# Another order of the steps up to the first scores in a cross-attention block

## The reference

```
q, kv = ln(x)*g_q + b_q, ln(ctx)*g_kv + b_kv
qp = q @ Wq.T + bq ; kp = kv @ Wk.T + bk ; vp = kv @ Wv.T + bv
scores = qh @ kh.T / sqrt(32) - spatial_scale[h]*dist(query_xy, token_xy) + spatial_offset[h]
scores = where(mask, scores, -inf)
x = x + softmax(scores) @ vh @ Wo.T + bo
h = ln(x)*g_m + b_m
return x + gelu(h @ W1.T + b1) @ W2.T + b2
```

## Time and profile before

| | us |
|---|---|
| median of 3 runs | 1246.89 (1246.64 to 1247.19) |
| the profiled execution's own time | 1248.32 |
| its span, first to last instruction | 1246.5 |
| TensorE busy | 1205.4 (97%) |
| VectorE busy | 995.8 (80%) |
| ScalarE busy | 855.0 (69%) |
| GpSimd busy | 1000.9 (80%) |
| mean granted TensorE clock | 0.994 |

### The profile page before, as it was taken

How to read it: one execution, slowest core, us unless ns; L and a number is a source line. 1 busy time by engine, 2 the same in 40 slices (tenths; PEclk the granted TensorE clock), 3 DMA queues, 4 the chain that set the end, 5 groups by cost and what they waited for, 6 DMA issues and landing times.

```text
span 1246.5 us, 27428 instructions
## 1 busy us (share of the span) xinstructions
PE 1205.4 (97%) x9258; PEld 782.5 (63%) x9258; DVE 995.8 (80%) x2656; ACT 855.0 (69%) x1918; POOL 1000.9 (80%) x1286
## 2 busy tenths in 40 slices
PE   7887889999999999999999999999999999999998
PEld 2333456666666666666666666666666676666664
DVE  6799998888888989888888987978888887778321
ACT  6877758776767667776767677776767776676331
POOL 5587989989898988979898998989898987768320
PEclk8999999999999999999999999999999999999999
DMA  8599999989899898989899998889999997779543
GB/s 236 156 201 204 246 205 203 203 184 208 198 207 217 180 212 188 212 190 202 195 208 215 179 226 187 198 195 205 201 204 206 195 211 176 167 176 176 145 115 122
DMA packets 469692, 241.67 MB, mean 194 GB/s; under 512 B 385056, under 2 KB 409904, under 8 KB 469552
## 3 DMA queue, kind: packets, MB, share of 16 engines
q1 hardware_dynamic: 469552, 239.93, 85.7%
HBM read 109.66 MB, written 12.58 MB: 98 GB/s over the span
## 4 chain that ended last, share of the span: by engine, by line
PE 83%; DVE 8%; POOL 2%; issue 2%; ACT 2%; DMA 2%; SPq 1%; POOLq 0%; DVEq 0%; ACTq 0%
PE ps_up L637 26%; PE ps_down L652 26%; PE ps_qk L573 11%; PE ps_vo L597 6%; PE ps_vo L594 6%; PE ps_s L608 4%; PE ps_pv L622 4%; DVE soft L1088 1%; DVE p_nat L1105 1%; DVE w L1039 1%; DVE stats L1051 1%; POOL p_nat L1282 0%; DMA c_stage<-in_w 0%; DMA stack<-stack 0%; SPq L375 0%
## 5 line engine op out<-in xcount | busy, mean ns | idle before, releaser
L1282 POOL TENSOR_SCALAR p_nat<-soft,row_inv 128x256 f16<-128x256 f32 x512 | 332.9, 660 | 58.5 <-DVE row_inv L1099 57.1
L637 PE MATMUL ps_up<-hT,w 128*128 128x256 f16 x3072 | 377.2, 273 | 1.8 <-issue 1.0
L652 PE MATMUL ps_down<-w,hid 128*128 128x512 f16 x1536 | 372.9, 379 | 0.6 <-DVE hid L1137 0.4
L637 PEld LDWEIGHTS ps_up<-hT,w 128*128 128x128 f16 x3072 | 300.3, 98 | 91.5 <-issue 2.8
L801 ACT ACTIVATE soft<-soft,neg_max 128x256 f32<-128x256 f32 x512 | 255.3, 500 | 129.9 <-DVE neg_max L1088 128.9
L1088 DVE CUSTOM_DVE_ANT_0 soft<-ps_s,soft,factor 128x256 f32<-128x256 f32 x512 | 225.6, 476 | 115.6 <-PE ps_s L608 115.2
L1105 DVE SCALAR_TENSOR_TENSOR p_nat<-soft,row_inv,p_nat 128x256 f16<-128x256 f32 x512 | 296.7, 619 | 1.9 <-POOL p_nat L1282 1.7
L1290 POOL TENSOR_SCALAR soft<-dist,scale_neg,offset 128x512 f32<-128x512 f32 x256 | 249.3, 974 | 12.6 <-DVE p_nat L1105 11.0
L652 PEld LDWEIGHTS ps_down<-w,hid 128*128 128x128 f16 x1536 | 148.6, 97 | 132.2 <-DMA w<-x_scratch 1.0
L834 ACT ACTIVATE u<-ps_up,bias,up_scale 128x256 f32<-128x256 f32 x256 | 142.5, 557 | 122.0 <-PE ps_up L637 121.7
L1298 POOL TENSOR_SCALAR hid<-u,hid_scale 128x1024 f16<-128x1024 f32 x64 | 78.2, 1223 | 100.6 <-ACT u L840 100.6
(11 more groups left out here) (127 smaller groups left out, 1532.1 us busy)
## 6 DMA issues: line engine op xcount, KB each, us to landing
w<-x_scratch SPq DMA_DIRECT2D x256, 256.0 KB, 3.1
stack<-qk_parts SPq DMA_DIRECT2D x256, 96.0 KB
raw<-in_ctx SPq DMA_DIRECT2D x32, 256.0 KB, 3.6
raw<-in_x SPq DMA_DIRECT2D x32, 256.0 KB, 3.1
c_stage<-in_w SPq DMA_DIRECT2D x32, 256.0 KB, 3.8
x<-in_x SPq DMA_DIRECT2D x32, 256.0 KB, 3.4
out<-x SPq DMA_DIRECT2D x32, 256.0 KB, 3.2
tok_rows<-in_tok_xy SPq DMA_DIRECT2D x16, 256.0 KB, 4.3
```

Of the source, the lines that this page charges most:

```text
L637: mm = e.matmul(ps_up[s % 2][:, 0:L], w_1_sb[:, wp, k, m * P:(m + 1) * P], hT[:, b % 2, :, xp * KT + k, :], start=(k, wp, xp) == (0, 0, 0) ...
L652: mm = e.matmul(ps_down[tt][:], hid[:, chunk % HID_RING, i, hp, tt * P:(tt + 1) * P], w_2_sb[:, s % W2_RING, wp, :], start=(m == 0 and (hp ...
L1282: mine = e.tensor_scalar(p_nat[:, nat, HI, lc, :], soft[:, ring, lc, :], row_inv[:, ring, lc:lc + 1], 1.0, ALU.mult, ALU.mult)
```

## The change

It moves steps to other slots, and within them to other places in the engines' order. Up to slot 0:

- SyncE: the bias row of W_k is turned into columns before the second tile is transposed and no more behind W_v's load; that of W_q just before the fourth tile; that of W_v in slot 2. W_o's load moves from slot -14 to slot -2, behind the first stack copies; `keep_mask` moves from slot -18, ahead of the chunk loads, to slot -4, behind the first of them.
- ScalarE: `bias_row` of W_k stands between the second and third quarter of W_q's squares; the distance squares of batch 0 move from slot -22, ahead of W_q's high part, to slot -5; W_v's square from slot -6, ahead of the query's high part, to slot -3; its high part from slot -3 to slot -1; W_o's square from slot -2 to slot 0 and its high part from slots 1, 2 to 2, 3. ScalarE issues two of the four first stack copies itself.
- VectorE: statistics and low parts of the first tiles interleave otherwise with the norms of W_k and W_q; the masks and the two score factors move behind the first key low part; W_v's low part moves from slot -3 to slot 0; W_o's by a slot.
- TensorE: W_v's bias matmuls move from slot -3 to slot 0, totals by some slots; fill matmuls: 14 for 12, and 8 more before the first scores.
- GpSimd: norms and the distance sum at the matching places.
- W_1's chunks, norms and parts go one slot later; W_2's stay in their slots.

`GAINED_Q` is the count of gains that W_q's high part and bias wait for; the score factors no longer belong to it.

```diff
+        GAINED_Q = GS[0] + 2
-        TOTAL = (-30, -28, -4, 0) + tuple(range(0, 32, 4))
-        NORM = (-28, -25, -3, 0) + tuple(range(1, 33, 4))
-        GAIN = (-27, -24, -3, 1) + tuple(range(2, 34, 4))
+        TOTAL = (-30, -26, -3, 1) + tuple(range(1, 17, 4)) + tuple(range(16, 32, 4))
+        NORM = (-28, -24, -2, 1) + tuple(range(2, 18, 4)) + tuple(range(17, 33, 4))
+        GAIN = (-26, -22, -1, 2) + tuple(range(3, 19, 4)) + tuple(range(18, 34, 4))
...
-            def stack_copies(G):
+            def stack_copies(G, heads=range(HPG)):
-                for j in range(HPG):
+                for j in heads:
...
-                for sec, at_slot in ((SEC_V, -25), (SEC_O, -14)):
+                for sec, at_slot in ((SEC_V, -25), (SEC_O, -2)):
                         load_weight(sec)
-                for sec, at_slot in ((SEC_K, -25), (SEC_Q, -24), (SEC_V, -1)):
+                for sec, at_slot in ((SEC_K, -26), (SEC_Q, -19), (SEC_V, 2)):
                         bias_turn(sec)
-                if slot == -18:
+                if slot == -4:
                     keep_mask()
-                    stack_copies(G)
+                    stack_copies(G, range(HPG // 2) if G == 0 else range(HPG))
-                for step in due(slot, -6, ITEM, 2 * N_CHUNKS * KT):
+                for step in due(slot, -5, ITEM, MT):
                     load_chunk(*divmod(step, KT))
+                for step in due(slot, MT - 6, ITEM, MT):
+                    load_chunk(*divmod(MT + step, KT))
...
-                for at_slot, count in ((-32, 10), (-30, 1), (-28, 1), (-8, 12), (-6, 6)):
+                for at_slot, count in ((-32, 10), (-30, 1), (-26, 1), (-8, 14), (-6, 6), (-2, 8)):
                         warm(count)
-                for sec, at_slot in ((SEC_K, -31), (SEC_Q, -29), (SEC_V, -3)):
+                for sec, at_slot in ((SEC_K, -31), (SEC_Q, -29), (SEC_V, 0)):
                         weight_bias(sec)
...
+            def stack_copies_first():
+                gate.wait_ge(s_qklo, n_qk(0, 1))
+                for j in range(HPG // 2, HPG):
+                    src = qk_parts[32 * j:32 * j + 32, :, :, :].rearrange("p r w l -> p r (w l)")
+                    e.dma_start(stack[0:96, 0, j, :, :].rearrange("p w l -> p (w l)"), src).then_inc(s_stack[0], DMA)
...
-                for sec, at_slot in ((SEC_K, -26), (SEC_Q, -24), (SEC_V, -2)):
+                for sec, at_slot in ((SEC_K, -29), (SEC_Q, -24), (SEC_V, 1)):
                         bias_row(sec)
-                for sec, at_slot in ((SEC_K, -25), (SEC_Q, -20), (SEC_V, -3)):
+                for sec, at_slot in ((SEC_K, -26), (SEC_Q, -20), (SEC_V, -1)):
                         weight_hi(sec, range(KT))
-                for half_of in due(slot, 1, ITEM, 2):
+                for half_of in due(slot, 2, ITEM, 2):
                     weight_hi(SEC_O, range(2 * half_of, 2 * half_of + 2))
-                for sec, at_slot in ((SEC_V, -6), (SEC_O, -2)):
+                for sec, at_slot in ((SEC_V, -3), (SEC_O, 0)):
                         weight_square(sec)
+                if slot == -4:
+                    stack_copies_first()
-                    if slot == -22:
+                    if slot == -5:
                         dist_square(0, c)
-                if slot == -4:
+                if slot == -3:
                     dist_sqrt(0)
-                for step in due(slot, -4, ITEM, 2 * N_CHUNKS * KT):
+                for step in due(slot, -3, ITEM, MT):
                     chunk_square(*divmod(step, KT))
-                for step in due(slot, 2, ITEM, MT):
+                for step in due(slot, 3, ITEM, MT):
                     w1_hi(*divmod(step, KT))
...
-                for w, at_slot in ((AT[SEC_K], -29), (AT[SEC_Q], -26), (AT[SEC_V], -5)):
+                for w, at_slot in ((AT[SEC_K], -29), (AT[SEC_Q], -25), (AT[SEC_V], -3)):
                         weight_sums(w)
                 if slot == -21:
                     bias_column(SEC_K)
+                if slot == -5:
                     masks()
-                if slot == -5:
-                    small_scale()
                     bias_column(SEC_Q)
+                    score_factors()
+                if slot == -4:
+                    small_scale()
-                for sec, pieces, at_slot in ((SEC_K, range(1), -26), (SEC_K, range(1, KT), -25), (SEC_Q, range(KT), -20),
-                                            (SEC_V, range(KT), -3)):
+                for sec, pieces, at_slot in ((SEC_K, range(1), -23), (SEC_K, range(1, KT), -22), (SEC_Q, range(KT), -21),
+                                            (SEC_V, range(KT), 0)):
                         weight_lo(sec, pieces)
-                for half_of in due(slot, 1, ITEM, 2):
+                for half_of in due(slot, 2, ITEM, 2):
                     weight_lo(SEC_O, range(2 * half_of, 2 * half_of + 2))
-                for step in due(slot, 3, ITEM, MT):
+                for step in due(slot, 4, ITEM, MT):
                     w1_lo(*divmod(step, KT))
```

More of the change, by code:

```diff
@@ L688, in tensor_program @@
                     clear_rows()
-                if slot == 4:
+                if slot == 5:
                     value_bias_out()
@@ L715, in tensor_program @@
                     taken += vo_done + (4 if due(slot, 1, ITEM, MT) else 0)
-                    taken += 16 if slot == 4 else 0
+                    taken += 16 if slot in (0, 5) else 0
                     keep_busy(ps_pv if slot < 9 else ps_down[0], max(0, SLOT_STEPS - taken))
@@ L726, in columns_square, with quarter_squares @@
                 e.activation(cols_sq[:], cols_sb[:], ACT.Square).then_inc(s_colsq)
-            def quarter_squares(sec):
-                for k in range(KT):
+            def quarter_squares(sec, quarters):
+                for k in quarters:
                     gate.wait_ge((s_wk if sec == SEC_K else s_wq)[k], DMA)
@@ L764, in weight_hi @@
             def weight_hi(sec, pieces):
-                gate.wait_ge(s_gs, GS[AT[sec]])
+                gate.wait_ge(s_gs, GAINED_Q if sec == SEC_Q else GS[AT[sec]])
                 for k in pieces:
@@ L881, in scalar_program @@
                         dist_square(b, c)
-                for step in due(slot, -4, ITEM, 2 * N_CHUNKS * KT):
+                if slot == -3:
+                    dist_sqrt(0)
+                for step in due(slot, -3, ITEM, MT):
                     chunk_square(*divmod(step, KT))
-                for step in due(slot, 2, ITEM, MT):
+                for step in due(slot, MT - 4, ITEM, MT):
+                    chunk_square(*divmod(MT + step, KT))
+                for step in due(slot, 3, ITEM, MT):
                     w1_hi(*divmod(step, KT))
@@ L966, in gains, with score_factors @@
                     e.tensor_tensor(hid_norm[:, 0, c:c + 1], mine, norm[:, AT_W1 + c:AT_W1 + c + 1], ALU.mult).then_inc(s_gs)
+            def score_factors():
+                key, query = slice(AT[SEC_K], AT[SEC_K] + 1), slice(AT[SEC_Q], AT[SEC_Q] + 1)
+                e.scalar_tensor_tensor(out=factor[:, 0:1], in0=norm[:, query], scalar=-SCORE_SCALE / A_SCALE ** 2,
+                                       in1=norm[:, key], op0=ALU.mult, op1=ALU.mult).then_inc(s_gs)
+                e.scalar_tensor_tensor(out=factor[:, 1:2], in0=inv[:, query], scalar=A_SCALE ** 2 / SCORE_SCALE,
+                                       in1=inv[:, key], op0=ALU.mult, op1=ALU.mult).then_inc(s_gs)
             def hidden_norm():
@@ L1152, in vector_program @@
                     inverse(k)
[L1153 removed]
+                for b, n in at_tile(slot, (-30, -29, -17, -17), (-30, -30, -28, -27), (1, 2, 4, 4), (9, 10, 15, 15)):
                     norm_stats(b, n)
                     norm_aggregate(b, n)
[L1156 removed]
+                for w, at_slot in ((AT[SEC_K], -29), (AT[SEC_Q], -25), (AT[SEC_V], -3)):
                     if slot == at_slot:
                         weight_sums(w)
[L1159 to L1161 removed]
+                for c in due(slot, 1, KT, N_CHUNKS):
+                    weight_sums(AT_W1 + c)
+                for c in due(slot, MT, KT, N_CHUNKS):
+                    weight_sums(AT_W2 + c)
+                for b, which in at_pair(slot, (-29, -17), (-30, -27), (2, 4), (10, 15)):
                     norm_eps(b, which)
@@ L1326, in gpsimd_program @@
                     norm_root(N_W)
-                for b, which in at_pair(slot, (-28, -16), (-30, -28), (3, 5), (11, 16)):
+                for b, which in at_pair(slot, (-28, -16), (-30, -27), (3, 5), (11, 16)):
                     norm_rstd(b, which)
-                for b, n in at_tile(slot, (-27, -24, -16, -15), (-30, -29, -28, -25), (3, 4, 5, 6), (11, 12, 16, 17)):
+                for b, n in at_tile(slot, (-27, -24, -16, -15), (-30, -29, -27, -23), (3, 4, 5, 6), (11, 12, 16, 17)):
                     norm_apply(b, n)
-                for b, n in at_tile(slot, (-20, -19, -11, -10), (-30, -29, -28, -25), (3, 4, 6, 7), (12, 13, 21, 22)):
```

(1 more changed line is left out.)

22 lines of the change are left out of this document (6 added, 16 removed).

## The result

| | before | after |
|---|---|---|
| median of 5 runs, us | 1246.89 (1245.91 to 1247.30) | 1251.84 (1250.67 to 1254.79) |
| the profiled execution | 1248.32 | 1250.67 |
| its span | 1246.5 | 1248.9 |
| mean granted clock | 0.994 | 0.995 |

The ratio is 1.0043 (95% interval 1.0032 to 1.0053): 4.95 us slower, where 0.4 was predicted. So I read the traces for places and causes, and the medians for prices. Every execution compared here was a fast one except one of f4's, which took 2091.41 us and is left out of its ratio and interval (f4's median is 1249.21 with it and 1249.08 without).

What follows compares the result with a forecast made beforehand. VectorE was taken to set the pace from 46.8 to 192 us, TensorE behind it. A 3.2 us lead at the first maximum shrinks to a 0.4 us loss: 1246.9 + 0.4 = 1247.3 us, range 1243.5 to 1250.0.

Steps and rivals of the forecast that it cites:

- Up to the first query low part: Kernel start: VectorE's reordering finishes the first query low part at 27.2 us, 3.8 us earlier than 31.01.
- The copies from ScalarE: First stack copies: two issued by ScalarE cost it 1.4 us and gain only two issues on SyncE, off the path.
- This part hides nothing: First stack copies: all four on SyncE would land near 32.9 us, while scores wait for something else until 33.
- To the fourth maximum: Through slot 1: first maximum at 34.7 us (3.2 ahead), second at 41.8 (0.8 ahead), fourth at 51.8.
- What costs nothing: W_o's load behind the copies, W_1's preparation a slot later, doubled slots and fewer slot 0 fill matmuls: priced at nothing.
- Rival B: ScalarE, full from the first query low part on, becomes the wall: slower, 1249.3 to 1250 us; chance 0.20.
- Rival C: First scores are not earlier, as W_v's total and fills precede them on TensorE; end at 1247 us; chance 0.10.
- Rival A: The 3.2 us lead at the first maximum is kept whole, giving 1243.7 us; chance 0.28 beyond 2.5 us.
- My bounds: Limits on the sum: -3.2 us to +2.4, up to 0.7 more if VectorE's pieces overlap GpSimd.

Runs made afterwards that it cites:

- f4: The changed kernel with W_v's square in slot -7, ahead of the query's high part; 1249.21 us, ratio 1.0020 to the kernel before.
- e1: The changed kernel with the total of W_1's second block ahead of the output-bias matmuls and key projection in slot 5; 1251.90 us, ratio 1.0033 to before.
- e3: The changed kernel with the output-bias matmuls back in slot 4 (columns in slot 3, sum in slot 5); 1249.51 us, ratio 1.0020 to before.
- f1: The changed kernel with 12 more fill matmuls at the end of slot 4; 1251.46 us, ratio 1.0035 to before.
- f2: The changed kernel with three quarters of the output-bias matmuls left out, the rest still in slot 5; 1249.19 us, ratio 1.0019 to before.
- e4: The changed kernel with all four first stack copies issued from SyncE, none from ScalarE; 1250.59 us, ratio 1.0024 to before.
- e2: The kernel before with only W_1's preparation a slot later and the output-bias matmuls in slot 5; 1248.70 us, ratio 1.0016 to before.
- g2: The kernel before with the new order up to the first query low part, W_1's preparation a slot later and output-bias matmuls in slot 5; 1247.61 us.
- g6: The kernel before with the new order up to the first query low part, and W_o's load right behind the mask row; 1244.09 us, ratio 0.9985.
- f3: The changed kernel with output-bias matmuls back in slot 4, all first copies from SyncE and W_v's square in slot -7; 1248.25 us, ratio 1.0008 to before.
- g1: The kernel before with only the new order up to the first query low part, everything for W_v, W_o, bias and W_1 in old slots; 1245.80 us.
- g4: The kernel before with the new order up to the first query low part, and W_o's load behind the first stack copies; 1248.98 us, ratio 1.0016.
- g3: The kernel before with the new order up to the first query low part, and the mask row issued by ScalarE; 1247.39 us, ratio 1.0003.
- g5: The kernel before with the new order up to the first query low part, but the mask computed and sent early; 1245.96 us, ratio 0.9994.

## Why the prediction was wrong

- *Up to the first query low part*: right in the profiled execution, 27.27 for 27.2, and the query projection kept the clock (1.47 us, not 2.72). One reserve: in the traces of e1 and e3, which have the same order up to there, that step starts at 29.06 and 28.71 instead of 26.79. There W_k's first eight bias matmuls take 5.18 and 5.46 us for 3.59, and VectorE waits 1.36 and 1.96 us for the total; in f1 and f2 the step starts at 27.13 and 26.89. The prediction put no term for the clock there. How often after's executions, which spread over 4.1 us, have this late front, and how much of its median it makes, was not separated.
- *The copies from ScalarE*: right in what they cost ScalarE, 1.31 us of issuing for the 1.4 said. That the whole of it reaches the end is less sure: the median of e4 gives 1.4, within the noise, and its trace 0.8. "This part hides nothing" holds only nearly: without it the first scores wait for the stack until 33.45.
- *To the fourth maximum*: right within 0.5 us at each point named, again in the profiled execution. The eight fill matmuls took 2.47 us for the 1.9 said. W_v's square behind the copies was in the sum and is the front's largest price (2.7 by the median of f4, 1.2 at its first two maxima); a part is shared with the clock of the bias matmuls.
- ***What costs nothing*: this step failed.** I put W_1's preparation a slot later at nothing "since VectorE is the bound all through", and did not list the output-bias matmuls at all, though the change has them a slot later (a line that the excerpt of the diff leaves out). Putting an edit at nothing on that ground needs the check that nobody makes VectorE wait. In slot 5 TensorE has 6.85 us of work between one maximum and the result that VectorE needs next; before, it had 3.6 + 0.3 there. The runs showed in place of the zero: 2.5 us (e3) and 2.7 (f2), and 1.6 to 1.8 for the whole shift in a kernel without the rest of the change (e2) or with its front alone (g2).
- *Rival B* had the right side and too small a size (1249.3 to 1250), and half of the mechanism: ScalarE was on the path, and its part is in f4 and perhaps e4; the clock loss came not in the query projection but in the bias matmuls, behind 3.16 us of idle TensorE. *Rival C* fell, first scores at 33.48. *Rival A* needed W_v's low part before 39 us; g6 does that and keeps a part of the lead.
- My bounds ended at +3.1 because each term of them was in the front; a zero has bounds too.

Left open: how the 4.95 us divide. The undone parts sum to more than their joint effect (2.5 + 1.4 + 2.7 for 3.7 in f3), so they hide behind each other, and each is a difference of medians that is good to 1.5 us or so. The traces, which differ by 2.35 us only, agree with the forecast's 0.4 plus the shift; what the medians have beyond that may be the late front of some executions, which no run isolates.

## What to carry to other kernels

When an edit shifts a step by a slot on one engine, add up that engine's work in the new slot between the event that starts it and the result that the bound engine takes next; "the other engine is the bound" is true only while that sum is shorter. Undo a price by moving the amount of work, not the instruction at which the wait shows. When compute is pulled earlier, list for each transfer the time at which it is used less the time that it takes to land, and issue them in the order of these latest starts, not of their uses: here the place of one load gave 1.8 us (g1 to g6, with overlapping intervals) or cost 2.4 (g1 to g4, just clear of each other).

## What the runs showed of the hardware

- An 8 KB transfer issued 2.66 us behind a 1 MB one, with two of 256 KB between, landed after 6.1 us (g1), and after 6.1 us too when another engine issued it (g3, three of 256 KB between). Behind the two of 256 KB without the megabyte it took 3.2 us (g4), and ahead of all of them 2.1 (before) and 1.9 (g5).
- Eight fp32 matmuls of 128x512 took 5.10 us in after, behind 3.16 us of idle TensorE and two short matmuls, with a granted clock of 0.50 from 64 to 66 us. They took 3.60 at a granted clock of 1.00 where fill matmuls had run up to 0.57 us before those (f1), but also behind 2.69 us of idle (f4); in e1, behind 2.71, they ran at 0.50 again (67 to 68 us). So the length of the idle time alone did not decide it here.
- Two transfers issued by ScalarE held it 1.31 us (27.30 to 28.61), and its next instruction began at 28.71. A megabyte took 5.5 to 6.0 us to land in before, g1 and g6, and 7.8 behind four copies of 96 KB and beside other loads (g4).
